# Self-attention with a fused 1x1 convolution: chunk 7's keys, chunk 6's and 7's scores and the turns of the maxima in another order

## The chip, the cores and the metric

One core of one Trainium2 chip runs the whole kernel. The metric is the device time of one execution in microseconds (us). TensorE does the matrix products into PSUM, VectorE (DVE) and ScalarE (ACT) copy, subtract and exponentiate, GpSimd (POOL) subtracts maxima, SyncE (SP) issues the transfers.

## What is computed

The input is four images of 256 channels and 64 x 64 = 4096 positions. The reference, cut to what matters:

```
xf = x.reshape(b, c, n)                     # 4, 256, 4096
q, k = Wq xf + bq, Wk xf + bk               # 32 channels each
v = Wv xf + bv                              # 256 channels
att = softmax(q^T k / sqrt(32), axis=-1)    # 4096 x 4096 per image
out = gamma * (v att^T)
result = Wf concat([out, x]) + bf           # 256 channels
```

All in float32. The kernel folds the first half of Wf and gamma into Wv, so that attention gives its part of the result at once, and computes the second half of Wf on x (the "convolution") while it reads x.

## The kernel before, in words

**Numbers in two parts.** Each float32 operand of a product is split into a high part, which a copy to a reduced format (fp32r) gives, and a low part, the rest, which DVE subtracts. A product is then three: high by high, high by low and low by high (`product3`). For keys and queries the parts are stacked on partitions, so that one product of 96 rows does all three.

**Two stages for each image.** `images` loops over the four images: projection of image 0, then a loop of three rounds (attention of image b, projection of image b + 1), then the attention of the last image. So the attention of image 0 follows the entry into the loop, those of images 1 and 2 follow the jump back to its head, that of image 3 follows the exit.

*Projection* goes over 8 chunks of 512 positions. A chunk has, on TensorE: the projection to keys and queries (6 products of 512 columns into `ps_p[:, 0]`), the four value tiles (each 6 products of 256 columns; tiles 0 and 1 into one bank of `ps_o`, tiles 2 and 3 into the other), two convolutions (6 products of 512 columns each), and one or two sets of "early scores". The other engines follow: ACT copies the high part of the next chunk's x (`split_x`), of keys and queries (`kq_hi`), of values (`values_out`), and stores the convolutions (`conv_out`); DVE makes the low parts (`split_x`, `kq_lo`, `values_lo`). `hi` and `lo` have two places, by chunk parity.

*Early scores.* A set of scores is four products of 256 columns (512 keys against a block of 256 queries), in two halves of two products. Each half takes one of three PSUM banks of `ps_s`. ACT copies it to `raw` (`keep_scores`), and then DVE folds it into a running maximum (`fold_scores`). On TensorE half h of `scores` waits until `max_done` has counted h - 2 folds, that is for the fold of half h - 3 (halves are numbered from 0), whose bank it takes; so three halves are under way at most. The sets are numbered in the order in which they are made (`MADE`): the set of chunk 6 has number 10 (halves 20 and 21), that of chunk 7 number 11 (halves 22 and 23).

*The maxima.* When all sets of block 0 are folded, `reduce_top` joins two running maxima to `top_j`; TensorE turns it into columns (`turn_top`, two transposes into `ps_t`); DVE reduces them to `top_col` (`reduce_turned`); TensorE turns and spreads that over all partitions (`spread_top`, two transposes); ACT copies it to `top_m` (`keep_top`); DVE subtracts it from the first slot of `raw` (`subtract_first`), and ACT makes the first exponential of it (`exponential_hi`), with which the attention begins. POOL subtracts it from the other slots.

*Attention* goes over 16 blocks of 256 queries, 8 steps each: per step 24 products of values with exponentials and 4 products of scores for 12 steps ahead.

**Order.** There is no planner. Each engine works through its own instructions in the order in which the code writes them, and semaphores, counted up by each piece, hold it: `k_out` and `q_out` tell that the low (and so both) parts of a chunk's keys and queries are there and that `ps_p[:, 0]` is free, `x_split` that a chunk's x is split, `v_free` that a bank of `ps_o` is free, `conv_ready` that a convolution is complete. The last convolution of chunk 7 goes into a bank of `ps_s`.

SP's queue: in chunk c it loads chunk c + 2 after the split of chunk c + 1 is done, then stores the two convolutions of chunk c.

Of the kernel before, what the change touches and what calls it, by code (L numbers as in the profile page):

```python
# [14 lines left out]
def attention_conv(nc, x, wkqT, wv, wf1T, wf2T, vectors, out):  # L15
# [4 lines left out]
    CHUNKS = N // W  # L20
    JT = N // P
    JC = W // P
# [30 lines left out]
    with ExitStack() as ctx:  # L53
# [163 lines left out]
        def _(pe):  # L217
# [70 lines left out]
            def project(b, c, first):  # L288
                C = snap(pe, b * CHUNKS + c)
                start = first and c == 0  # L290
                finishing = not first and c == 0
                last_chunk = c == CHUNKS - 1

                def project_kq(c, C):
                    pe.wait_ge(x_split, C + 1)
                    product3(ps_p[:, 0], lambda k: wkq_hi[:, k], lambda k: wkq_lo[:, k],
                             lambda k: x_hi(c)[:, k, :], lambda k: x_lo(c)[:, k, :]).then_inc(kq_ready, 1)

                def convolve(dst, ot, halfway=None):
                    product3(dst, lambda k: wf2_hi[:, k, ot * P:(ot + 1) * P],  # L300
                             lambda k: wf2_lo[:, k, ot * P:(ot + 1) * P],
                             lambda k: x_hi(c)[:, k, :], lambda k: x_lo(c)[:, k, :], halfway).then_inc(conv_ready, 1)

                def project_values(j):
                    if j % 2 == 0:
                        pe.wait_ge(v_free, C * 2 + (j // 2 + 1))
                    last = product3(ps_o[:, j // 2, (j % 2) * C_IN:(j % 2 + 1) * C_IN],
                                    lambda k: x_hi(c)[:, k, j * P:(j + 1) * P], lambda k: x_lo(c)[:, k, j * P:(j + 1) * P],
                                    lambda k: wvf_hi[:, k], lambda k: wvf_lo[:, k])
                    if j % 2:  # L310
                        last.then_inc(v_ready, 1)

                def early_scores(q):
                    scores(b * HALVES, MADE[q], 2 * MADE[q] % BANKS, q % QUADS, q // QUADS)

                if last_chunk:
                    pe.wait_ge(k_out, C + 1)
                    early_scores(c)
                    for j in range(JC):
                        project_values(j)  # L320
                    turn_top(b * BLOCKS, None)
                    pe.wait_ge(q_out, C + 1)
                    convolve(ps_p[:, 0], 0, lambda: spread_top(b * BLOCKS))
                    convolve(ps_s[:, LAST_CONV].rearrange("p j i -> p (j i)"), 1)
                    return
                if start:
                    warm_up()
                    pe.wait_ge(wkq_split, 1)
                elif finishing:
                    pe.wait_ge(lo_done, b * STEPS)  # L330
                else:
                    pe.wait_ge(k_out, C)
                project_kq(c, C)
                if start:
                    fold_weights()
                    pe.wait_ge(wf2_split, 1)
                    convolve(ps_t[:], 0)
                    pe.wait_ge(wvf_split, 1)
                    pe.wait_ge(ones_done, 1)
                if finishing:  # L340
                    turn_out(b * BLOCKS)
                project_values(0)
                project_values(1)
                if not start:
                    if finishing:
                        pe.wait_ge(finished, b * BLOCKS)
                    else:
                        pe.wait_ge(conv_done, C * 2)
                    convolve(ps_t[:], 0)
                project_values(2)  # L350
                project_values(3)
                pe.wait_ge(k_out, C + 1)
                pe.wait_ge(q_out, C + 1)
                if c in BETWEEN:
                    early_scores(BETWEEN[c])
                if c == CHUNKS - 2:
                    early_scores(c)
                    project_kq(c + 1, C + 1)
                    convolve(ps_p[:, 1], 1)
                else:  # L360
                    convolve(ps_p[:, 1], 1)
                    early_scores(c)

            def attend(b, n, r, last_image):
                B = snap(pe, b * BLOCKS + n)
# [78 lines left out]
        def _(act):  # L444
# [21 lines left out]
            def project(b, c, first):  # L466
# [26 lines left out]
                def early_scores(q):  # L493
                    keep_scores(b * HALVES, MADE[q], 2 * MADE[q] % BANKS, q)

                if last_chunk:
                    early_scores(c)
                    conv_out(ps_p[:, 1], 1, C - 1)
                    values_out(0)
                    values_out(1)  # L500
                    keep_top(b * BLOCKS, 0)
                    conv_out(ps_p[:, 0], 0)
                    act.wait_ge(sub0_done, b + 1)
                    exponential_hi(0, 0)
                    act.wait_ge(conv_done, C * 2 + 1)
                    exponential(b * STEPS, 0, 0)
                    conv_out(ps_s[:, LAST_CONV].rearrange("p j i -> p (j i)"), 1)
                    return
                if start:
                    split_x(0, 0)  # L510
                    act.wait_ge(wf2_loaded, 16)
                    nc.scalar.activation(wf2_hi[:], wf2_raw, ACT.Copy).then_inc(wf2_hi_done, 1)
                    act.wait_ge(vec_loaded, 16)
                    act.wait_ge(bkq_spread, 1)
                kq_hi(c, C)
                if start:
                    act.wait_ge(wvf_ready, 1)
# [3 lines left out]
                    act.wait_ge(pv_done, b * STEPS)  # L521
                elif not start:
                    act.wait_ge(conv_ready, C * 2)
                split_x(b, c + 1)
                values_out(0)
                conv_out(ps_t[:], 0)
                values_out(1)
                if c in BETWEEN:
                    early_scores(BETWEEN[c])
                if c == CHUNKS - 2:  # L530
                    early_scores(c)
                    kq_hi(c + 1, C + 1)
                else:
                    conv_out(ps_p[:, 1], 1)
                    early_scores(c)

            def exponential_hi(t, slot):
                nc.scalar.activation(hi[:, t % 2], raw[:, slot].rearrange("p j i -> p (j i)"), ACT.Exp,  # L538
# [34 lines left out]
        def _(dve):  # L573
# [83 lines left out]
            def project(b, c, first):  # L657
# [22 lines left out]
                    fold_scores(b * HALVES, MADE[q], 2 * MADE[q] % BANKS, None if q % QUADS == 0 else q // QUADS, q // QUADS)  # L680

                if last_chunk:
                    early_scores(c)
                    reduce_top(b * HALVES + 2 * MADE[c] + 2)
                    values_lo(0)
                    reduce_turned(b * BLOCKS)
# [8 lines left out]
                if finishing:  # L695
                    normalise(b * BLOCKS - 1, 1)
                    add_conv(b * BLOCKS - 1, 0, b * (16 * USES[0]))
                kq_lo(c, C)
                if start:
                    setup_values()  # L700
                split_x(C + 1, c + 1)
                values_lo(0)
                values_lo(1)
                if c in BETWEEN:
                    early_scores(BETWEEN[c])
                early_scores(c)
                if c == CHUNKS - 2:
                    kq_lo(c + 1, C + 1)

            def attend(b, n, r, last_image):  # L710
                B = snap(dve, b * BLOCKS + n)
# [98 lines left out]
```

## Time and profile before

| | us |
|---|---|
| median of 3 runs (2033.78 to 2034.09) | 2033.83 |
| the profiled execution, its own time | 2033.3 |
| its span, first to last instruction | 2031.4 |
| TensorE products busy | 2015.3 (99%) |
| TensorE weight loads busy | 1980.4 (97%) |
| ScalarE busy | 1748.9 (86%) |
| VectorE busy | 1584.9 (78%) |
| GpSimd busy | 1206.1 (59%) |

The 16 transfer engines move 34 GB/s on average. Two thirds of the chain of work that ended last are products of values in the attention. The projections of the four images lie at about 3 to 75, 514 to 579, 1018 to 1084 and 1523 to 1588 us. Products are pipelined, and their recorded durations overlap, so the distance between two starts is what one costs in a dense stretch.

### The profile page before, as it was taken

How to read it: one execution, taken by the hardware profiler on the slowest of the kernel's cores; microseconds unless marked ns; L12 is line 12 of the kernel's file. 1: busy time of each engine (PE TensorE's matmuls, PEld its weight loads, DVE VectorE, ACT ScalarE, POOL GpSimd, SP SyncE). 2: the span in 40 equal slices, each digit the busy share in tenths (PEclk: the TensorE clock that was granted, in tenths of full speed). 3: DMA queues.
4: the chain of work that ended last, by engine and by line, in shares of the span. 5: the costliest groups of instructions: out<-in, count | busy, mean ns of one | idle time of the engine just before them, and what ended most of it. 6: DMA issues, size and time to landing. Idle time of an engine off the chain costs nothing.

```text
span 2031.4 us, 45017 instructions
## 1 busy us (share of the span) xinstructions
PE 2015.3 (99%) x16232; PEld 1980.4 (97%) x16232; DVE 1584.9 (78%) x2157; ACT 1748.9 (86%) x2373; POOL 1206.1 (59%) x514
## 2 busy tenths in 40 slices
PE   9999999999999999999999999999999999999999
PEld 8999999999899999999989999999998999999999
DVE  6788888886778888888677888888867788888885
ACT  7888888887888888888788888888878888888886
POOL 0467766667056677666605666766660666677665
PEclk9999999999999999999999999999999999999999
DMA  4200000000310000000031000000003100000000
GB/s 136 84 22 22 15 15 21 21 21 12 120 70 22 22 21 15 16 21 21 11 125 65 22 21 21 21 10 21 21 11 130 38 22 21 21 21 18 13 21 17
DMA packets 54081, 69.46 MB, mean 34 GB/s; under 512 B 4048, under 2 KB 37584, under 8 KB 53968
## 3 DMA queue, kind: packets, MB, share of 16 engines
q1 hardware_dynamic: 53696, 67.91, 10.0%
q8 instruction: 68, 1.11, 0.2%
q14 instruction: 45, 0.37, 0.1%
q10 hardware_dynamic: 272, 0.07, 0.0%
HBM read 34.41 MB, written 33.55 MB: 33 GB/s over the span
## 4 chain that ended last, share of the span: by engine, by line
PE 92%; DVE 3%; ACT 3%; issue 2%; DMA 0%; DVEq 0%; ACTq 0%; SPq 0%
PE ps_o L388 72%; PE ps_s L380 11%; PE ps_p L242 3%; PE ps_o L242 2%; PE ps_t L284 1%; ACT queries L478 1%; ACT hi L453 1%; DVE val_lo L676 1%; PE ps_s L259 1%; PE ps_t L276 1%; PE ps_t L269 1%; DVE top L612 1%; DVE lo L599 1%; PE ps_t L242 0%; DVE raw L626 0%
## 5 line engine op out<-in xcount | busy, mean ns | idle before, releaser
L755 POOL TENSOR_TENSOR raw<-raw,top_m 128x1024 f32<-128x1024 f32 x508 | 1205.4, 2413 | 809.1 <-ACT top_m L464 809.1
L631 DVE TENSOR_TENSOR lo<-ps_p,hi 128x1024 fp32r<-128x1024 f32 x512 | 626.9, 1224 | 311.4 <-ACT ps_p L545 311.1
L612 DVE TENSOR_TENSOR top<-ps_s,top 128x512 f32<-128x512 f32 x960 | 660.0, 687 | 55.6 <-ACT raw L459 7.4
L538 ACT ACTIVATE hi<-raw 128x1024 fp32r<-128x1024 f32 x512 | 543.9, 1062 | 145.9 <-PE ps_o L388 141.4
L388 PE MATMUL ps_o<-val_hi,hi 128*128 128x258 f32 x4096 | 664.5, 284 | 4.1 <-ACT hi L538 4.1
L388 PE MATMUL ps_o<-val_lo,hi 128*128 128x256 f32 x4096 | 652.4, 281 | 0.0
L459 ACT ACTIVATE raw<-ps_s 128x512 f32<-128x512 f32 x1024 | 554.1, 595 | 54.7 <-PE ps_s L380 32.0
L388 PE MATMUL ps_o<-val_hi,lo 128*128 128x258 f32 x4096 | 599.3, 284 | 0.0
L388 PEld LDWEIGHTS ps_o<-val_hi,hi 128*128 128x128 f32 x4096 | 562.4, 189 | 5.8 <-issue 4.6
L388 PEld LDWEIGHTS ps_o<-val_lo,hi 128*128 128x128 f32 x4096 | 560.4, 189 | 0.0
L388 PEld LDWEIGHTS ps_o<-val_hi,lo 128*128 128x128 f32 x4096 | 538.7, 190 | 0.0
L545 ACT ACTIVATE ps_p<-raw 128x1024 f32<-128x1024 f32 x512 | 516.7, 1009 | 0.0
L380 PE MATMUL ps_s<-queries,keys 96*128 (+1 forms) x1856 | 306.7, 287 | 0.0
L380 PEld LDWEIGHTS ps_s<-queries,keys 96*128 96x128 f32 x1856 | 253.9, 190 | 0.1
L242 PE MATMUL ps_o<-wvf_hi,hi 128*128 128x256 f32 x256 | 72.0, 281 | 0.2 <-DVE bias L593 0.2
L242 PE MATMUL ps_o<-wvf_hi,lo 128*128 128x256 f32 x256 | 71.6, 280 | 0.0
L242 PE MATMUL ps_o<-wvf_lo,hi 128*128 128x256 f32 x256 | 71.5, 279 | 0.0
L643 DVE TENSOR_SCALAR o_norm<-ps_o,inv 128x256 f32<-128x256 f32 x128 | 61.9, 484 | 6.3 <-DVE inv L639 1.1
L242 PEld LDWEIGHTS ps_o<-wvf_hi,hi 128*128 128x128 f32 x256 | 48.0, 188 | 3.0 <-DVE bias L593 0.6
L242 PEld LDWEIGHTS ps_o<-wvf_lo,hi 128*128 128x128 f32 x256 | 48.1, 188 | 2.3
L649 DVE TENSOR_TENSOR result<-ps_t,result 128x512 f32<-128x512 f32 x64 | 43.6, 681 | 5.8 <-PE ps_t L284 5.8
L242 PEld LDWEIGHTS ps_o<-wvf_hi,lo 128*128 128x128 f32 x256 | 48.0, 188 | 0.0
(72 smaller groups left out, 1028.3 us busy)
## 6 DMA issues: line engine op xcount, KB each, us to landing
xf<-x SPq DMA_DIRECT2D x32, 512.0 KB, 3.7
conv_d<-conv_st SPq DMA_DIRECT2D x64, 256.0 KB, 2.0
result<-conv_d SPq DMA_DIRECT2D x64, 256.0 KB, 2.6
out<-result SPq DMA_DIRECT2D x64, 256.0 KB, 2.2
raw<-wf2T SPq DMA_DIRECT2D x1, 256.0 KB, 3.9
raw<-wv SPq DMA_DIRECT2D x1, 256.0 KB, 4.3
raw<-wf1T SPq DMA_DIRECT2D x1, 256.0 KB, 4.7
raw<-wkqT ACTq DMA_DIRECT2D x1, 64.0 KB, 2.0
```

What stands on the lines that cost most here:

```text
L242: last = nc.tensor.matmul(dst, a(k), b(k), start=(i == 0), stop=(i == len(terms) - 1))
L259: last = nc.tensor.matmul(ps_s[:, (bank + half) % BANKS, jl], keys[:, j * P:(j + 1) * P], queries[:, bass.ds(n * I, I)], start=True, stop= ...
L380: last = nc.tensor.matmul(ps_s[:, (2 * (QUADS * r + a) + half) % BANKS, jl], keys[:, j * P:(j + 1) * P], queries[:, bass.ds((n + a // QUAD ...
L388: last = nc.tensor.matmul(ps_o[:, i, 0:width], p[:, t % 2, jl * I + i * P:jl * I + (i + 1) * P], v[:, j, 0:width], start=opens and jl == 0 ...
L459: nc.scalar.activation(raw[:, slot, 2 * half:2 * half + 2], ps_s[:, (bank + half) % BANKS], ACT.Copy).then_inc(raw_done, 1)
L538: nc.scalar.activation(hi[:, t % 2], raw[:, slot].rearrange("p j i -> p (j i)"), ACT.Exp, scale=SCALE).then_inc(hi_done, 1)
L545: nc.scalar.activation(ps_p[:].rearrange("p h n -> p (h n)"), raw[:, slot].rearrange("p j i -> p (j i)"), ACT.Exp, scale=SCALE).then_inc(p ...
L612: nc.vector.tensor_tensor(top[:, new], scores, top[:, new if half else old], ALU.max).then_inc(max_done, 1)
L631: nc.vector.tensor_tensor(lo[:, t % 2], ps_p[:].rearrange("p h n -> p (h n)"), hi[:, t % 2].bitcast(F32), ALU.subtract).then_inc(lo_done, 1)
L643: nc.vector.tensor_scalar(o_norm[:, i], ps_o[:, i, 0:C_IN], inv[:, i:i + 1], None, ALU.mult).then_inc(o_scaled, 1)
L649: nc.vector.tensor_tensor(result[:, r], ps_t[:].rearrange("p (k n) -> p k n", k=KT), result[:, r], ALU.add).then_inc(finished, 1)
L755: nc.gpsimd.tensor_tensor(raw[:, slot], raw[:, slot], top_m[:, r].unsqueeze(1).broadcast_to((P, JQ, I)), ALU.subtract).then_inc(sub_done, 1)
```

## The change

All of it is in `project`, that is in the stage of projection, on TensorE, ACT and DVE. The counts and shapes of all operations stay.

In chunk 6, on TensorE: after the first convolution it waits for both parts of chunk 6's keys and queries, then comes chunk 7's projection, chunk 6's scores, value tiles 2 and 3, chunk 7's scores, and the second convolution. Before, value tiles 2 and 3 came right after the first convolution, then chunk 6's scores, chunk 7's projection and the second convolution; chunk 7's scores opened chunk 7.

In chunk 7, on TensorE: the turn of `top_j` stands between value tiles 1 and 2, the spreading of `top_col` behind tile 3, and both convolutions follow. Before, the turn stood behind tile 3 and the spreading half-way through the first convolution.

ACT and DVE take chunk 7's split in front of chunk 6's keys and queries, chunk 7's keys and queries in front of chunk 6's scores, and chunk 6's second pair of value tiles between the two sets of scores.

```
@@ TensorE, chunk 7
-                    pe.wait_ge(k_out, C + 1)
-                    early_scores(c)
-                    for j in range(JC):
-                        project_values(j)
+                    project_values(0)
+                    project_values(1)
                     turn_top(b * BLOCKS, None)
+                    project_values(2)
+                    project_values(3)
+                    spread_top(b * BLOCKS)
                     pe.wait_ge(q_out, C + 1)
-                    convolve(ps_p[:, 0], 0, lambda: spread_top(b * BLOCKS))
+                    convolve(ps_p[:, 0], 0)
                     convolve(ps_s[:, LAST_CONV].rearrange("p j i -> p (j i)"), 1)
@@ TensorE, the other chunks, behind the first convolution
+                if c == CHUNKS - 2:
+
+                    pe.wait_ge(k_out, C + 1)
+                    pe.wait_ge(q_out, C + 1)
+                    project_kq(c + 1, C + 1)
+                    early_scores(c)
+                    project_values(2)
+                    project_values(3)
+                    pe.wait_ge(k_out, C + 2)
+                    early_scores(c + 1)
+                    convolve(ps_p[:, 1], 1)
+                    return
                 project_values(2)
                 project_values(3)
                 pe.wait_ge(k_out, C + 1)
                 pe.wait_ge(q_out, C + 1)
                 if c in BETWEEN:
                     early_scores(BETWEEN[c])
-                if c == CHUNKS - 2:
-                    early_scores(c)
-                    project_kq(c + 1, C + 1)
-                    convolve(ps_p[:, 1], 1)
-                else:
-                    convolve(ps_p[:, 1], 1)
-                    early_scores(c)
+                convolve(ps_p[:, 1], 1)
+                early_scores(c)
@@ ACT
                 if last_chunk:
-                    early_scores(c)
                     conv_out(ps_p[:, 1], 1, C - 1)
...
+                if c == CHUNKS - 2:
+                    act.wait_ge(conv_ready, C * 2)
+                    split_x(b, c + 1)
                 kq_hi(c, C)
...
-                split_x(b, c + 1)
+                if c < CHUNKS - 2:
+                    split_x(b, c + 1)
                 values_out(0)
                 conv_out(ps_t[:], 0)
+                if c == CHUNKS - 2:
+                    kq_hi(c + 1, C + 1)
+                    early_scores(c)
+                    values_out(1)
+                    early_scores(c + 1)
+                    return
                 values_out(1)
                 if c in BETWEEN:
                     early_scores(BETWEEN[c])
-                if c == CHUNKS - 2:
-                    early_scores(c)
-                    kq_hi(c + 1, C + 1)
-                else:
-                    conv_out(ps_p[:, 1], 1)
-                    early_scores(c)
+                conv_out(ps_p[:, 1], 1)
+                early_scores(c)
@@ DVE
                 if last_chunk:
-                    early_scores(c)
                     reduce_top(b * HALVES + 2 * MADE[c] + 2)
...
+                if c == CHUNKS - 2:
+                    split_x(C + 1, c + 1)
                 kq_lo(c, C)
                 if start:
                     setup_values()
-                split_x(C + 1, c + 1)
+                if c < CHUNKS - 2:
+                    split_x(C + 1, c + 1)
                 values_lo(0)
+                if c == CHUNKS - 2:
+                    kq_lo(c + 1, C + 1)
+                    early_scores(c)
+                    values_lo(1)
+                    early_scores(c + 1)
+                    return
                 values_lo(1)
                 if c in BETWEEN:
                     early_scores(BETWEEN[c])
                 early_scores(c)
-                if c == CHUNKS - 2:
-                    kq_lo(c + 1, C + 1)
```

## Rows read from the trace of the kernel before

**Rows 1.** The page: busy time and share; the span in 40 slices, in tenths

```profile
PE 2015.3 (99%) x16232; PEld 1980.4 (97%) x16232; DVE 1584.9 (78%) x2157; ACT 1748.9 (86%) x2373; POOL 1206.1 (59%) x514
...
PE   9999999999999999999999999999999999999999
...
PEclk9999999999999999999999999999999999999999
```

**Rows 2.** Timeline, TensorE, image 0: start, us, engine, line, operation [idle before]

```profile
58.70 0.39 PE L242 MATMUL ps_p<-hi,wkq_hi 128*128 128x512 f32 x1
...
62.91 0.28 PE L242 MATMUL ps_o<-wvf_hi,hi 128*128 128x256 f32 x1
...
64.80 0.47 PE L242 MATMUL ps_p<-hi,wkq_hi 128*128 128x512 f32 x1
...
68.26 0.73 PE L259 MATMUL ps_s<-queries,keys 96*128 96x256 f32 x4 [0.43 <-DVE keys L665]
...
71.66 0.38 PE L269 MATMUL ps_t<-ident,top_j 128*128 128x128 f32 x2
...
72.57 0.42 PE L276 MATMUL ps_t<-ident,top_col 128*128 128x128 f32 x2
...
73.53 0.39 PE L242 MATMUL ps_s<-hi,wf_hi 128*128 128x512 f32 x1
...
75.89 0.76 PE L388 MATMUL ps_o<-val_hi,hi 128*128 128x258 f32 x4 [0.80 <-ACT hi L538]
```

**Rows 3.** The same timeline, ACT

```profile
58.63 1.08 ACT L459 ACTIVATE raw<-ps_s 128x512 f32<-128x512 f32 x2
60.29 0.68 ACT L475 ACTIVATE keys<-ps_p,bkkqq 64x512 fp32r<-64x512 f32 x1 [0.58 <-PE ps_p L242]
61.00 1.37 ACT L478 ACTIVATE queries<-ps_p,bkkqq 32x512 fp32r<-32x512 f32 x2
...
64.55 0.60 ACT L490 ACTIVATE val_hi<-ps_o 128x512 fp32r<-128x512 f32 x1
65.02 1.10 ACT L459 ACTIVATE raw<-ps_s 128x512 f32<-128x512 f32 x2
...
73.03 0.38 ACT L464 ACTIVATE top_m<-ps_t 128x256 f32<-128x256 f32 x1 [0.57 <-PE ps_t L276]
...
74.70 1.06 ACT L538 ACTIVATE hi<-raw 128x1024 fp32r<-128x1024 f32 x1 [0.28 <-DVE raw L626]
```

**Rows 4.** The same timeline, DVE

```profile
62.41 0.75 DVE L669 SCALAR_TENSOR_TENSOR queries<-ps_p,bkkqq,queries 32x512 fp32r<-32x512 f32 x1 [0.66 <-ACT queries L478]
...
64.74 1.29 DVE L676 TENSOR_TENSOR val_lo<-ps_o,val_hi 128x512 fp32r<-128x512 f32 x2
65.95 1.48 DVE L612 TENSOR_TENSOR top<-ps_s,top 128x512 f32<-128x512 f32 x2
...
70.95 0.42 DVE L617 TENSOR_TENSOR top_j<-top 128x256 f32<-128x256 f32 x1
...
72.08 0.42 DVE L621 TENSOR_REDUCE top_col<-ps_t 128x2 f32<-128x256 f32 x1
...
73.44 1.22 DVE L626 TENSOR_TENSOR raw<-raw,ps_t 128x1024 f32<-128x1024 f32 x1 [0.26 <-ACT top_m L464]
```

**Rows 5.** Load of chunk 7 of image 0: SP's timeline; issues with us to landing

```profile
50.80 0.43 SPq L160 DMA_DIRECT2D xf<-x  x1
...
xf<-x SPq DMA_DIRECT2D x1, 512.0 KB, 4.6
```

**Rows 6.** Timeline, TensorE's weight loads, the second half of chunk 5's scores

```profile
58.36 0.30 PEld L259 LDWEIGHTS ps_s<-queries,keys 96*128 96x128 f32 x2 [0.32 <-DVE top L612]
```

**Rows 7.** Timeline of image 1, TensorE and ACT, where its attention begins

```profile
578.77 0.40 PE L242 MATMUL ps_s<-hi,wf_lo 128*128 128x512 f32 x1
...
580.41 0.76 PE L388 MATMUL ps_o<-val_hi,hi 128*128 128x258 f32 x4 [1.24 <-ACT hi L538]
...
578.76 1.06 ACT L538 ACTIVATE hi<-raw 128x1024 fp32r<-128x1024 f32 x1 [0.20 <-DVE raw L626]
```

## The prediction

> **What bounds the kernel now.** The page first: TensorE is busy 99% of the span [rows 1]. I therefore ask of every edit one thing: at what time does TensorE begin the attention of the image, its long dense part? Work that is moved costs nothing and gives nothing unless that time moves. The change leaves the count and the shapes of all instructions as they are; only orders change, in chunks 6 and 7 of each of the four images.
>
> Next the timeline of the first image from chunk 6 on, one engine at a time [rows 2 to 4]. "A pair of value tiles" below is 12 products of 256 columns, "a convolution" and "the projection" are 6 products of 512 columns each. TensorE starts chunk 6's projection at 58.70 and the attention at 75.89, 17.19 us. The pieces: from 58.70 to 62.91 a projection, a pair and a convolution (4.21), from there to 64.80 a pair and the four score products (1.89; I take 1.41 and 0.48), so projection and convolution are 1.40 each. The whole of the two chunks is two projections, four convolutions, four pairs, two sets of scores and the two turns (0.14 and 0.18, my reading of what follows the rows at 71.66 and 72.57): 8.4 + 5.6 + 1.0 + 0.3 = 15.3 us. So 1.9 us are pauses, and they are: chunk 7's scores, which could have begun at 64.80 + 0.07 + 2 x 1.40 = 67.67 and begin at 68.26 when DVE has made the low part of the keys (0.6); the attention, which could have begun at 73.53 + 1.40 = 74.93 and begins at 75.89 when ACT has the first exponential (1.0); the rest is small seams. That, less than 2 us in an image, is all that this change can win.
>
> **The change part by part, first image.** Prices: raw copies of two score halves 1.10, the first of them done 0.60 after it starts and the second starting 0.50 after it; queries 1.37, keys 0.68, hi copy 1.06 (by the exponential, which has its shape), value copy 0.60 with the next start after 0.47 [rows 3]; on DVE queries 0.75 (the keys' low part has the same shape), two folds 1.48, so 0.69 for the first, two value subtractions 1.29 (0.65 each), top_j 0.42, column maxima 0.42, the 128x1024 subtraction 1.22 [rows 4]. Handing over from one engine to the next is some 0.05; a product's result is there 0.16 after the place at which the next could start (0.39 of the last minus its 0.23).
>
> *The split of chunk 7, moved ahead of chunk 6's keys.* ACT ends chunk 5's raw copies at 59.71 [rows 3], so the hi copy runs 59.7 to 60.8, keys to 61.5, queries 61.5 to 62.9. The convolution of chunk 5 that it waits for is long over by then, and the chunk's load was issued at 50.80 and such a load landed in 4.6 [rows 5], so nothing is added. DVE's 1.22 for the split lie beside ACT's keys and queries; its low part of the queries follows the copies, 62.9 to 63.7. In front of these copies everything is 0.5 later than before (the queries' copies began at 61.00).
>
> *Chunk 7's projection, moved ahead of the value tiles 2 and 3.* It overwrites the same PSUM bank, so it waits for that low part of the queries: ready at 62.91, it starts at 63.7. **Pause of 0.8 us**, new: before, 1.41 of value tiles and 0.48 of scores covered it. TensorE then runs projection and scores of chunk 6 to 65.6 and the pair to 67.0.
>
> *Chunk 7's scores in front of the second convolution.* Three PSUM banks hold scores, and the code lets a half start once the half three before it is folded and its bank so free (the max_done wait in scores). The halves of chunk 7 are numbers 22 and 23; 23 wants the fold of number 20, the first half of chunk 6. Follow that one: the projection is complete at 65.3; ACT now does chunk 7's keys (65.3 to 66.0) and queries (to 67.4) *before* it copies chunk 6's scores, so raw 20 is there at 68.0; DVE is in the low part of the queries until 68.15 and folds 20 until 68.9. TensorE has the keys in time (66.8), does half 22 from 67.0 to 67.2, and stands before half 23 until 68.95. **Pause of 1.7 us**, new. Convolution and value tiles are queued behind it, in order, and the score copy of 23, hence the maxima, too. That such a wait really holds TensorE is in the trace: chunk 5's second half stood 0.32 for exactly this releaser, the fold of the half three before [rows 6].
>
> *What is no longer between the turns.* From 68.95: half of the scores, the convolution and the first pair, to 72.0. DVE: fold 21 to 69.7, value tile to 70.3, folds 22 and 23 to 71.8, top_j to 72.2; the first turn starts at 72.3 (**pause 0.3**). Tiles 2 and 3 end at 73.8. Column maxima: ACT copies the first pair at 72.2 to 72.8, DVE subtracts it until 73.5, then reduces until 73.9; the second turn at 73.9 to 74.1 (**pause 0.1**). Two convolutions end at 74.1 + 2.81 = 77.0 with a seam.
>
> *The first exponential.* Before, second turn to top_m took 0.46, top_m to DVE's subtraction 0.41, that 1.22, and the exponential 1.06 with the hand-overs: 72.57 to 75.89, 3.3 in all [rows 2 to 4]. Now ACT and DVE have the second pair of value tiles in between (ACT until 74.5, DVE until 75.3; before, the low values were done before top_m). So top_m at 74.5 to 74.9, subtraction 75.3 to 76.5, exponential 76.6 to 77.6, attention at **77.7** instead of 75.89: **+1.8 us**. The change takes away the 0.6 at the keys and 0.2 of the 1.0 before the attention, and puts in 0.8, 1.7, 0.3 and 0.1: by pauses +2.1, less some seams; the two ways agree within 0.3, and I take 1.8 as it follows the last wait.
>
> *The other images.* Image 3 looks like image 0. Images 1 and 2 begin with the jump back to the head of the loop over images: in image 1 the exponential is done at 579.82, the last product starts at 578.77, and attention starts only at 580.41, 1.64 after that product starts, 1.41 after its place in the queue is free [rows 7]. There the start follows the end of the second convolution, 77.0 against 74.93, plus the same 1.41: **+2.0 us**. The exponential (77.6 on the clock of image 0, against 78.4) stays hidden. [...]
>
> Nothing is given back later. TensorE is dense after 75.89, and the exponentials of the next steps stand in the same distance to the start as before. Stores of the convolutions are issued up to 2 us later, and their results are wanted tens of us on.
>
> **Sum**: 2 x 1.8 + 2 x 2.0 = 7.6 us. Profiled execution 2033.3 to 2040.9; the median of the runs is 0.5 above it, so 2033.83 + 7.6 = **2041.4 us**, +0.37%.
>
> **The rivals.**
> Forecast, as worked out, chance 0.86. Its own range: hand-overs and overlapping tails (0.1 here and there over some ten steps) make 0.3 to 0.5 in an image, so 2039.5 to 2043.5.
> (a) *Only one pause counts*, 0.06. If ACT, which gets its conditions early, had the raw copy of half 20 a microsecond sooner than I schedule, the 1.7 shrinks to 0.7 and each image loses about 0.8 to 1.0: 2033.83 + 3.6 = 2037.4, at the edge of "same". For it: tails overlap on ACT (raw half starts 0.5 after the other). Against: keys and queries on ACT are 2.05 in one row after the other, with no overlap.
> (b) *The other sign*, 0.04: the fold of half 20 comes before TensorE asks. It decides whether that fold ends before 67.2, 1.7 earlier than I find, and then TensorE would have no hole at the keys and the turns hidden under convolutions. The gain is what pauses there are: 0.6 + 1.0 in images 0 and 3, and 0.6 in 1 and 2 where the jump remains, 4.4 together: 2029.4. What speaks against it is the order on ACT, raw copies behind keys and queries, and that fold and projection wait for nothing that could be early.
> (c) *It is absorbed*, 0.02: later starts are caught up in attention, 2034. TensorE is at 9 tenths in all slices [rows 1], there is nothing to catch up with.
> (d) *The clock*, 0.02. [...]
>
> **The numbers.** A measurement of this kernel can tell about 0.2% (4.1 us) from no change. Slower by more: forecast, (d) and a little of (a), 0.88. Within it: most of (a), (c), 0.08. Faster: (b), 0.04. Range, 8 in 10: below down to (a)'s 2037.5, above by the upper end of the step errors plus half a microsecond an image for seams I can't see, 2044.
>
> **What would show it.** In the profile after: a wait of TensorE of some 0.7 to 0.8 before a product into ps_p, released by DVE's low part of the queries; a wait of ps_s for DVE top near 1.7 in each image, the largest new one; the wait for DVE keys gone; top_col and top_j with waits of 0.1 to 0.3; the attention of image 0 at 77.7. I am wrong if the wait for the fold is under 1 us, if the attention starts before 76.5, or if waits of the same size turn up within the attention.

## The result, and the profile after

| | before | after |
|---|---|---|
| median of the runs, us | 2033.95 | 2042.12 |
| lowest to highest | 2033.78 to 2034.09 | 2042.01 to 2042.24 |
| span of the profiled execution | 2031.4 | 2040.1 |

The changed kernel is slower, by 8.2 us: ratio 1.004, 95% interval 1.0027 to 1.0053. The forecast was 2041.4 with a range of 2037.5 to 2044.0, so the sign and the size were right. By the spans of the two profiled executions the difference is 8.7, as the one of before (2033.3 us) is 0.65 below the median of its kernel.

The timeline of the changed kernel in image 0, TensorE; it answers to [rows 2]. In this execution chunk 6 starts at 58.81 and not at 58.70, so everything is 0.1 later than in the one of before ahead of the change.

```profile
63.70 0.47 PE L242 MATMUL ps_p<-hi,wkq_hi 128*128 128x512 f32 x1 [0.51 <-issue]
...
67.07 0.40 PE L259 MATMUL ps_s<-queries,keys 96*128 96x256 f32 x2
69.02 0.51 PE L259 MATMUL ps_s<-queries,keys 96*128 96x256 f32 x2 [1.55 <-DVE top L625]
...
72.26 0.44 PE L269 MATMUL ps_t<-ident,top_j 128*128 128x128 f32 x2
...
74.08 0.43 PE L276 MATMUL ps_t<-ident,top_col 128*128 128x128 f32 x2
...
77.83 0.75 PE L396 MATMUL ps_o<-val_hi,hi 128*128 128x258 f32 x4 [0.51 <-ACT hi L551]
```

The lines show the two new holes. Chunk 7's projection could have started at 63.02, 0.23 behind the last product ahead of it, and starts at 63.70, when DVE has the low part of chunk 6's queries (62.85 + 0.75 below): a hole of 0.7. The second half of chunk 7's scores, number 23, starts at 69.02 and not 0.24 behind the first at 67.07: from 67.31 the engine stands for 1.7 us. The idle time in brackets is 1.55, as it counts from the recorded end of the last product, 67.47. The wait is put down to DVE's fold. The next fence has the same stretch on ACT and then on DVE, for [rows 3, 4].

```profile
66.09 1.37 ACT L486 ACTIVATE queries<-ps_p,bkkqq 32x512 fp32r<-32x512 f32 x2
67.48 1.08 ACT L467 ACTIVATE raw<-ps_s 128x512 f32<-128x512 f32 x2
...
74.64 0.38 ACT L472 ACTIVATE top_m<-ps_t 128x256 f32<-128x256 f32 x1
...
76.64 1.06 ACT L551 ACTIVATE hi<-raw 128x1024 fp32r<-128x1024 f32 x1
...
62.85 0.75 DVE L682 SCALAR_TENSOR_TENSOR queries<-ps_p,bkkqq,queries 32x512 fp32r<-32x512 f32 x1
...
68.27 1.49 DVE L625 TENSOR_TENSOR top<-ps_s,top 128x512 f32<-128x512 f32 x2
...
71.78 0.42 DVE L630 TENSOR_TENSOR top_j<-top 128x256 f32<-128x256 f32 x1
...
75.39 1.21 DVE L639 TENSOR_TENSOR raw<-raw,ps_t 128x1024 f32<-128x1024 f32 x1
```

ACT copies chunk 7's queries from 66.09 and starts the score copies only behind them, at 67.48, so the first is there at about 68.08. DVE makes the low part of the queries from 67.49 to 68.24 and folds from 68.27; the first fold ends at 68.96, 0.06 before half 23. The waits of the whole run, who waited for whom (total, times, longest):

```profile
PE ps_s L259 <- DVE top L625: 6.2, 4, 1.6
...
ACT hi L551 <- POOL raw L774: 2.8, 2, 1.5
```

The first is the new hole, once in each of the four images. The second was not forecast; it belongs to the attentions of images 1 and 2. Image 1 in the timeline of the changed kernel, TensorE and then ACT (for [rows 7]):

```profile
582.87 0.40 PE L242 MATMUL ps_s<-hi,wf_lo 128*128 128x512 f32 x1
583.95 0.74 PE L396 MATMUL ps_o<-val_hi,hi 128*128 128x258 f32 x4 [0.69 <-ACT hi L551]
...
587.78 0.75 PE L396 MATMUL ps_o<-val_hi,hi 128*128 128x258 f32 x4 [0.21 <-ACT hi L551]
...
590.55 0.51 PE L388 MATMUL ps_s<-queries,keys 96*128 96x256 f32 x2 [0.35 <-DVE top L625]
...
584.50 0.67 ACT L494 ACTIVATE conv_st<-ps_s,bias 128x512 f32<-128x512 f32 x1
586.66 1.06 ACT L551 ACTIVATE hi<-raw 128x1024 fp32r<-128x1024 f32 x1 [1.49 <-POOL raw L774]
```

and the kernel before at the same place, ACT, then TensorE:

```profile
580.67 0.67 ACT L486 ACTIVATE conv_st<-ps_s,bias 128x512 f32<-128x512 f32 x1
582.10 1.06 ACT L538 ACTIVATE hi<-raw 128x1024 fp32r<-128x1024 f32 x1 [0.75 <-issue]
...
583.88 0.65 PE L388 MATMUL ps_o<-val_hi,hi 128*128 128x258 f32 x4
```

The second exponential of the attention is the first instruction of ACT behind the jump to the head of the loop. Before, it started 1.43 after the convolution's copy and was done at 583.16, in time for TensorE's second step at 583.88. After, it starts 2.16 behind the copy, is done at 587.72, and TensorE's second step, 3.47 behind the first in the kernel before, comes 3.83 behind it. The scores of that step then wait 0.35 for a fold of DVE (590.55), and behind them the whole 1.0 is lost: the next products start at 590.89 and before at 586.33, 4.56 apart, where the attentions start 3.54 apart. That POOL is named is no proof: POOL's subtraction for this slot began at 581.16 and takes 2.4, so it was done three microseconds before.

**Where 8.7 us of span went**, from the start of an attention and the start of the next projection (75.89, 513.78, 580.41, 1018.34, 1085.03, 1523.10, 1589.22 before; 77.83, 515.71, 583.95, 1022.91, 1091.07, 1529.94, 1597.93 after). Projections until the attention starts: +1.94, +1.61, +1.47, +1.87. Attentions: 0.0, +1.03, +0.80, 0.0. Together 8.7.

### The profile page after: what moved, and what is told of

It reads as the page before. It is cut to its first block, busy times and chain, and to the rows that moved or that the text cites. A ratio compares the mean times of both kernels' runs of the same rounds, so it can differ in the third digit from the quotient of the medians.

```text
span 2040.1 us, 45018 instructions
## 1 busy us (share of the span) xinstructions
PE 2018.3 (99%) x16232; PEld 1981.4 (97%) x16232; DVE 1584.6 (78%) x2157; ACT 1748.6 (86%) x2373; POOL 1205.9 (59%) x514
## 3 DMA queue, kind: packets, MB, share of 16 engines
q8 instruction: 68, 1.11, 0.2%
## 4 chain that ended last, share of the span: by engine, by line
PE 92%; ACT 3%; DVE 3%; issue 2%; DMA 0%; ACTq 0%; DVEq 0%; SPq 0%
PE ps_o L396 72%; PE ps_s L388 11%; PE ps_p L242 3%; PE ps_o L242 2%; PE ps_t L284 1%; ACT queries L486 1%; ACT hi L461 1%; PE ps_t L242 1%; PE ps_t L269 1%; DVE lo L612 1%; PE ps_s L259 1%; PE ps_t L276 1%; DVE val_lo L689 1%; DVE top L625 0%; DMA xf<-x 0%
## 5 line engine op out<-in xcount | busy, mean ns | idle before, releaser
L242 PE MATMUL ps_o<-wvf_hi,hi 128*128 128x256 f32 x256 | 72.3, 282 | 0.2 <-DVE bias L606 0.2
L689 DVE TENSOR_TENSOR val_lo<-ps_o,val_hi 128x512 fp32r<-128x512 f32 x64 | 42.3, 688 | 8.3 <-ACT val_hi L498 6.9
```

What stands on the lines that cost most here:

```text
L242: last = nc.tensor.matmul(dst, a(k), b(k), start=(i == 0), stop=(i == len(terms) - 1))
L689: nc.vector.tensor_tensor(val_lo[:, j2, :], ps_o[:, h].rearrange("p (j c) -> p j c", j=2), val_hi[:, j2, 0:C_IN].bitcast(F32), ALU.subtrac ...
```

## The experiments

The kernel before ran on the same chips, with medians of 2033.88 to 2034.02. The names are those of the first kernel's stages; "the changed kernel" is the one of the diff.

**1. Chunk 7's scores behind the second convolution.** Does TensorE's hole of 1.7 us cost 1.7 us?

```
                     pe.wait_ge(k_out, C + 2)      # moved, with early_scores(c + 1),
+                    convolve(ps_p[:, 1], 1)       # behind the convolution
                     early_scores(c + 1)
```

> The changed kernel, with chunk 7's scores behind chunk 6's second convolution on TensorE. Theory 1 (the chain through the queues of ACT and DVE sets the start of the attention, and TensorE's long pause only shows it): half 23 starts at about 69.0 as before this edit, because the fold of half 20 is no earlier; the pause of 1.7 shrinks to 0.3, but an equal one of about 1.6 appears before the turn of top_j, and the attention of image 0 starts at 77.5 to 77.8; total 2041 to 2042. Theory 2 (TensorE's pause is the loss): 1.4 us come back in each image, total about 2036.5.

Measured: 2041.76 us (ratio to before 1.0037, 1.0024 to 1.0051). The hole did shrink, and came back in front of the turn, where TensorE now waits for top_j:

```profile
72.32 0.44 PE L269 MATMUL ps_t<-ident,top_j 128*128 128x128 f32 x2 [1.38 <-DVE top_j L630]
```

The attention of image 0 starts at 77.89. Removing the longest wait of TensorE brought 0.4 us in all, hardly more than the scatter of the runs (2041.55 to 2042.20 here, 2042.01 to 2042.24 for the changed kernel). By the traces images 0 and 3 gain nothing (from projection to attention 77.89 and 68.01, where the changed kernel has 77.83 and 67.99); what there is lies in images 1 and 2, behind the jump. What sets the end is the chain over ACT's and DVE's queues; the hole only shows where TensorE meets it.

**2. Chunk 7's queries last on ACT and DVE.** The same chain, cut at its cause. `kq_hi` and `kq_lo` are divided into keys and queries:

```
@@ ACT, chunk 6
-                    kq_hi(c + 1, C + 1)
+                    k_hi(c + 1, C + 1)
                     early_scores(c)
                     values_out(1)
                     early_scores(c + 1)
+                    q_hi(c + 1, C + 1)
@@ DVE: k_lo in chunk 6; in chunk 7
                     reduce_top(b * HALVES + 2 * MADE[c] + 2)
+                    q_lo(c, C)
```

> The changed kernel, with chunk 7's queries taken on ACT behind both sets of scores and on DVE behind top_j; TensorE's order as it is. Theory 1 (the fold of half 20 is late because its raw copy is queued behind the 1.4 us of query copies): half 20 is folded at 67.5 instead of 69.0, the pause before half 23 is 0.3, top_j at 70.8, the attention of image 0 at about 76.3 (77.83 in the changed kernel, 75.89 before); total about 2036. Rival (the fold waits for something else, the projection or DVE's own queue): the pause stays over 1 us and the total at 2041 or more.

Measured: 2036.50 us (1.0011, 1.0002 to 1.0020): 5.6 of the 8.2 us come back. TensorE, then DVE, image 0:

```profile
67.70 0.50 PE L259 MATMUL ps_s<-queries,keys 96*128 96x256 f32 x2
70.95 0.44 PE L269 MATMUL ps_t<-ident,top_j 128*128 128x128 f32 x2
...
76.53 0.74 PE L396 MATMUL ps_o<-val_hi,hi 128*128 128x258 f32 x4 [0.50 <-ACT hi L554]
...
66.95 1.49 DVE L628 TENSOR_TENSOR top<-ps_s,top 128x512 f32<-128x512 f32 x2
```

The fold starts at 66.95 instead of 68.27, half 23 at 67.70 instead of 69.02, both 1.32 earlier, and the attention 1.30 earlier. One delay runs through the chain undiminished. The edit moved two things at once, ACT's copies of the queries (1.37) and DVE's low part of them (0.75); what each of them costs alone was not measured. In the changed kernel DVE's part ended last (68.24, the raw copy at 68.08), but it had waited for ACT's copies to end.

**3 and 4. The loop over images written out**, in the changed kernel and in the one before. No engine jumps between a projection and an attention:

```
-            with eng.Fori(0, IMAGES - 1) as b:
+            for b in range(IMAGES - 1):
```

> The changed kernel with the loop over images written out, so that no engine jumps back between the projection and the attention of images 1 and 2. Theory 1 (the jump delays TensorE's start and ACT's second exponential of the attention): images 1 and 2 behave as image 0; the losses within the attention (1.0 and 0.8 us found between its start and the next projection) go, and 0.25 at each start; total about 2040. Rival (these losses come from the later start itself, as from the transfers that now meet): they stay, total 2042.

> The kernel before with the loop over images written out. Theory 1: the attentions of images 1 and 2 start when the exponential is there, 0.5 to 0.6 earlier each: total about 2032.8. Rival (longer code costs reads of instructions elsewhere, or the 1.4 us were no jump): 2034 or more.

Measured: 2038.92 us for the changed kernel (1.0022, 1.0013 to 1.0031) and 2031.59 for the one before (0.9987, 0.9978 to 0.9996), 1 us better than expected in both. The attentions of images 1 and 2, from their start to the next projection, take 437.96 and 437.97 in the changed kernel written out, where they took 438.96 and 438.87; the one before takes 437.94 in both. ACT, image 1 of the changed kernel written out:

```profile
584.23 0.67 ACT L494 ACTIVATE conv_st<-ps_s,bias 128x512 f32<-128x512 f32 x1
584.80 1.05 ACT L551 ACTIVATE hi<-raw 128x1024 fp32r<-128x1024 f32 x1
```

The second exponential starts 0.57 behind the copy, where it was 2.16 with the loop. So the time lost within the attention belonged to the jump. The attention of image 0 speaks for the jump itself and not for anything else in the loop's code: it is that same code, entered without a jump, and takes 437.8 to 437.9 in every kernel with the loop. Without jumps the change costs 7.3 us instead of 8.2, and it costs nearly the same in each image: the attention starts 1.86, 1.78, 1.77 and 1.77 later, counted from the projection. That is the 1.8 which the prediction had for image 0.

**5. Value tiles 2 and 3 back in front of chunk 7's projection.** The other hole, in front of that projection:

```
                 if c == CHUNKS - 2:
+                    project_values(2)
+                    project_values(3)
                     pe.wait_ge(k_out, C + 1)
                     pe.wait_ge(q_out, C + 1)
                     project_kq(c + 1, C + 1)
                     early_scores(c)
-                    project_values(2)
-                    project_values(3)
```

> The changed kernel with value tiles 2 and 3 of chunk 6 back in front of chunk 7's projection on TensorE, so that they cover the wait for the low part of the queries. Theory 1 (the chain from chunk 7's projection over ACT's and DVE's queues to the first exponential sets the start): the pause of 0.5 to 0.8 before that projection goes, but the projection starts at 64.3 instead of 63.7, and everything behind it is 0.6 later, the attention of image 0 at 78.4; total about 2044.5. Theory 2 (each pause of TensorE is a loss of its own): 0.7 us come back in each image, total about 2039.

Measured: 2049.99 us (1.0080, 1.0066 to 1.0094). The sign is that of theory 1, the size is of neither. TensorE, image 0, and the windows of that stretch (busy time and count of each engine, granted clock, share and rate of transfers):

```profile
67.72 0.50 PE L259 MATMUL ps_s<-queries,keys 96*128 96x256 f32 x2 [1.07 <-DVE keys L677]
69.84 0.79 PE L259 MATMUL ps_s<-queries,keys 96*128 96x256 f32 x2 [1.62 <-DVE top L624]
70.43 0.63 PE L242 MATMUL ps_p<-hi,wf_hi 128*128 128x512 f32 x1
70.86 0.63 PE L242 MATMUL ps_p<-lo,wf_hi 128*128 128x512 f32 x1
...
75.55 0.50 PE L269 MATMUL ps_t<-ident,top_j 128*128 128x128 f32 x2
```

```profile
64.00:70.00 6.00, 3.31 (x20) 2.62 (x18) 2.76 (x5) 3.97 (x8) 0.00 (x0) 0.91 0.12 44
70.00:76.00 6.00, 6.00 (x23) 5.42 (x24) 2.89 (x5) 1.87 (x4) 0.00 (x0) 0.52 0.12 44
```

The chain is late by a little more than the 0.6 expected: half 23 starts at 69.84, 0.8 behind the changed kernel. But the products behind it start 0.43 apart instead of 0.233. The granted clock of this stretch is 0.52, where it is 1.00 over 58 to 64 and over 76 to 82 us. The wider distance lasts until about 75.6, and the convolution and two value tiles between 70.43 and 75.55 took 5.1 us instead of 2.8. Ahead of that it had stood 1.07 and 1.62, with two products in between. Images 2 and 3 have such a stretch too, of some 3 us (0.57 and 0.72 in windows of 4 and 6 us). Image 1 has not, though its two waits are the same (1.14 and 1.55; 1.15 and 1.55 in image 2, 1.14 and 1.55 in image 3). In image 1 it is 68.95 from the start of the projection to that of the attention, 0.7 more than the 68.24 of the changed kernel: 4 x 0.7 on 2042 is 2045, near what theory 1 expected. Images 0, 2 and 3 are later by another 2.6, 1.7 and 1.1 in the same stage, and these 5.4 us go with the lower clock.

**6. The turns alone, on the kernel before.**

```
-                    for j in range(JC):
-                        project_values(j)
+                    project_values(0)
+                    project_values(1)
                     turn_top(b * BLOCKS, None)
+                    project_values(2)
+                    project_values(3)
+                    spread_top(b * BLOCKS)
                     pe.wait_ge(q_out, C + 1)
-                    convolve(ps_p[:, 0], 0, lambda: spread_top(b * BLOCKS))
+                    convolve(ps_p[:, 0], 0)
```

> The kernel before with this part of the change alone: the turn of top_j between value tiles 1 and 2, the spreading behind tile 3. From the rows of before: top_j is ready at 71.4 and TensorE at 70.2, a pause of 1.2; spreading at 73.0 (72.57 before), then ACT and DVE have the second pair of value tiles in front of top_m and of the subtraction, attention of image 0 at about 76.8, +0.9; in images 1 and 2, where the jump hides half of it, +0.45. Total 2034 + 2.7 = about 2036.7. Rival (the turns cost nothing where they are put, as the waits that they meet are short): 2034.

Measured: 2038.46 us (1.0023, 1.0014 to 1.0032), 4.5 more than before, where 2.7 was expected. TensorE waits 1.02 for top_j, the spreading comes at 73.22, and the attention of image 0 starts at 77.10, 1.2 later than before. It was expected to cost 0.9 in two images and 0.45 in two. By the traces it costs 1.2, 1.5, 1.3 and 1.1: in images 1 and 2 only 0.6 of it shows at the start of the attention, and another 0.9 and 0.7 are lost behind the jump, where nothing was expected.

**7. The spreading back into the convolution, in the changed kernel.**

```
-                    spread_top(b * BLOCKS)
                     pe.wait_ge(q_out, C + 1)
-                    convolve(ps_p[:, 0], 0)
+                    convolve(ps_p[:, 0], 0, lambda: spread_top(b * BLOCKS))
```

> The changed kernel with the spreading of the maxima back half-way in the first convolution of chunk 7, at about 74.5 instead of 74.08 in image 0. For the jump: if TensorE's start behind it counts from the last wait that TensorE passes (3.8 us after the spreading in both kernels), the attention of image 1 starts 0.5 later than in the changed kernel, at 584.4; if it counts from the end of the last convolution, it starts at 583.9 as there. The first exponential waits for DVE's second value tile in any case, so image 0 stays within 0.1 of 77.83. Total 2042 to 2042.5.

Measured: 2041.85 us (1.0039, 1.0024 to 1.0055). The attention of image 1 starts at 584.06, with the spreading at 580.77, so 3.3 behind it and not 3.8: the start does not count from the last wait. (Image 0, expected within 0.1 of 77.83, starts at 78.00.) But nor does it keep a fixed distance to the last product, which is 1.64 and 1.70 before and 1.08 and 1.00 after.

**8. An order made by the chain, loop written out.** Taken from kernel 2 of this list (that of experiment 2), with the following on TensorE, and the other queues as the expectation says:

```
@@ chunk 6
                     project_values(2)
                     project_values(3)
                     pe.wait_ge(k_out, C + 1)
                     pe.wait_ge(q_out, C + 1)
                     project_kq(c + 1, C + 1)
                     early_scores(c)
                     convolve(ps_p[:, 1], 1)
                     pe.wait_ge(k_out, C + 2)
                     early_scores(c + 1)
@@ chunk 7
                     project_values(3)
                     turn_top(b * BLOCKS, None)
                     spread_top(b * BLOCKS)
```

> An order made by the chain: loop over images written out; on TensorE value tiles 2 and 3 of chunk 6, chunk 7's projection, chunk 6's scores, the second convolution as cover for chunk 7's keys, chunk 7's scores, its four value tiles, both turns, both convolutions; ACT and DVE take chunk 7's queries behind both sets of scores, DVE the column maxima before the value tiles and the first subtraction before the last. Theory 1: no pause at the keys, 0.3 before half 23, top_j at 70.8 instead of 71.4 and the attention of image 0 at 75.4 (75.89 before, 75.80 with the loop written out); total about 2030. Rival (the chain has another step that I don't see, and nothing comes of it): 2031.6 as the written-out loop alone, or more.

Measured: 2031.57 us (0.9988, 0.9979 to 0.9997), the same as the kernel before with the loop written out. The maxima came earlier, and another instruction took the gain. Its ACT, image 0:

```profile
72.81 0.39 ACT L471 ACTIVATE top_m<-ps_t 128x256 f32<-128x256 f32 x1 [0.32 <-PE ps_t L276]
74.22 0.69 ACT L494 ACTIVATE conv_st<-ps_p,bias 128x512 f32<-128x512 f32 x1 [1.02 <-PE ps_p L242]
74.80 1.05 ACT L553 ACTIVATE hi<-raw 128x1024 fp32r<-128x1024 f32 x1
```

DVE's subtraction is done at 74.45, and the exponential could start at 74.5, but ACT had begun the copy of the convolution, which this order made late enough to be in the way. The attention starts at 75.90, where 75.4 was expected and the kernel before written out has 75.80; this copy cost 0.3 of the 0.5 that are missing. It was not tried to turn these two round: the low part of the same exponential would wait for that copy.

**9. The rest of the change alone.** The changed kernel with both turns where they were.

```
-                    turn_top(b * BLOCKS, None)
                     project_values(2)
                     project_values(3)
-                    spread_top(b * BLOCKS)
+                    turn_top(b * BLOCKS, None)
                     pe.wait_ge(q_out, C + 1)
-                    convolve(ps_p[:, 0], 0)
+                    convolve(ps_p[:, 0], 0, lambda: spread_top(b * BLOCKS))
```

> The changed kernel with the turns of the maxima where they were before (behind tile 3, and half-way in the first convolution): the rest of the change alone. From the rows of the changed kernel: half 23 still starts at 69.0, the value tiles end at 73.6, turn at 73.6, top_col at 74.5, spreading at 74.6, top_m to 75.4, subtraction and exponential after it, attention of image 0 at 77.9 to 78.0. The turns alone cost 4.5 us in all. If the parts add up, the rest alone costs the other 3.7: total about 2037.7. If each part fills the other's wait (both chains end in the same first exponential), it costs as much as the whole: about 2042.

Measured: 2041.13 us (1.0039, 1.0025 to 1.0053), 7.2 over the kernel before. The attention of image 0 starts at 77.70. Turns 4.5, rest 7.2, both 8.2: the two delays lie beside each other, they don't add. Images 1 and 2 are worth a look here. Their attentions start 2.0 and 1.9 later than before, counted from the projection, 1.79 and 1.67 behind the start of the last product, and take 437.93 and 438.03: nothing is lost within them. So with the turns in their old places the kernel does what the prediction said of the jump. In all seven kernels here with the loop and the turn of top_j between value tiles 1 and 2, these attentions take 438.3 to 439.0. Why the place of the turn should matter to what comes behind the jump is not shown.

**10. Queries last, and value tiles back.** Kernel 2 with the edit of kernel 5.

> Chunk 7's queries last on ACT and DVE, as in the run that brought the most back, and value tiles 2 and 3 of chunk 6 back in front of chunk 7's projection, as in the run in which TensorE's clock fell. The chain: projection at 64.4, keys' low part at 67.5, fold of half 20 at 68.2, half 23 at 68.3 (67.70 without the tiles moved back), turn 71.6, attention of image 0 at 77.1; pauses of 1.2 and 0.5 us instead of 1.1 and 1.6. If the clock fell because of the long pauses close together, it stays at 1.00 here and the total is about 2038.7; if the place of the value tiles itself brings it down, the clock falls here too and the total is 2045 or more.

Measured: 2040.42 us (1.0034, 1.0022 to 1.0046), with runs from 2038.48 to 2041.70, wider than any other kernel's here. The profiled run is the 2038.48 one: half 23 at 68.18, turn at 71.43, attention at 77.01, 0.1 to 0.2 ahead of the expected times, and the granted clock is 1.00 over 60 to 80 us. So in this execution, with waits of 1.07 and 0.22, the clock held, and the time is the 2038.7 expected for that case. The other five are 1.3 to 3.2 us longer, and the two longest (2041.48 and 2041.70) have a mean clock of 0.998 against 0.999. That would fit a clock that falls in one or two images, but no trace shows it; the median lies between the two expectations and decides for neither.

**11. The turns alone, loop written out.**

> The turns alone, with the loop over images written out. If the 0.9 us which the attentions of images 1 and 2 lose behind a later start come from the jump, they go, and the cost of the turns is 1.2 us in each image and nothing else: 2031.6 (the kernel before written out) + 4.8 = 2036.4. If they come from something that the late turns disturb, about 2038.

Measured: 2036.10 us (1.0011, 1.0002 to 1.0020), 4.5 over the kernel before written out. The attentions take 437.96 and 437.96 again, and start 1.2, 1.1, 1.1 and 1.1 later than there with what went before taken off.

## Why the prediction was right

*The hole before chunk 7's projection, 0.8.* Right in place and cause: the projection starts at 63.70, forecast 63.7. As 0.1 was there before, the hole is 0.7.

*The hole before half 23, 1.7, by the fold of half 20.* Right in place, cause and size: 69.02, forecast 68.95. The cause (raw copies queued behind the query copies) is shown by experiment 2, which took the queries out of both queues and moved the fold and half 23 and the attention by the same 1.3.

*Turns and first exponential.* Turn 72.26 (72.3), spreading 74.08 (73.9), exponential 76.64 (76.6), attention 77.83 (77.7), of which 0.1 was there before the change. The two small waits ahead of the turns were 0.1 each, where 0.3 and 0.1 were forecast. That image 0 costs 1.8 was no luck: with the loop written out all four images cost 1.8 to 1.9 (experiments 3 and 4). The two ways of adding up, by waits and by the last wait, were put side by side in the prediction, as they agreed within 0.3, and it took the second. Experiments 1 and 5 say that they are not equals: a wait of TensorE that is taken away comes back in front of the next thing that the chain delivers (1), or delays the chain (5). Only the sum along the chain is a forecast.

*Images 1 and 2.* Here a step failed. The prediction took 1.41 us from the end of the last convolution to the attention as a constant, +2.0 at each start, and said that nothing would be lost within the attention. Measured were +1.6 and +1.5 at the starts, and 1.0 and 0.8 lost behind them, as ACT came back from the jump 2.2 and 2.0 after the copy instead of 1.4 and 1.6. Kernels 3 and 4 show that it is the jump, and kernel 9 that the constant holds as long as the turns are where they were. The prediction's own sign of being wrong, new waits within the attention, did turn up there: 1.5 and 1.3 on ACT, and 0.2 to 0.4 on TensorE. The term was 4.0 for both images and measured 4.9; that is most of the difference between 7.6 and 8.2 or 8.7 us. The range held it, with its half a microsecond an image for what could not be seen; the reason itself was not foreseen.

*The rivals.* That one hole alone counts, that the delay is absorbed, or that the kernel is faster: none happened. The clock did not fall in the changed kernel, whose single long wait is 1.55, with 1.00 in the windows of all four projections. In experiment 5 it did fall, to 0.52 over 70 to 76 us of image 0: 2.8 us of products took 5.1 there, and the attention started another 2.6 us later.

**Open.** What in the jump makes ACT late by 2.2 rather than 1.4, and what TensorE's start behind it counts from. Experiment 7 excluded both simple rules; experiment 9 ties it to the place of the turns, without a reason. Also what takes TensorE's clock down in three of four images of kernel 5 and not in the other, with the same two waits.

## What to carry to other kernels

Where the dense engine has pauses of 1 to 2 us in a hand-written order, find the chain of the other engines' queues that sets the next dense stretch, and add up along it. The longest wait of the dense engine is where it meets that chain; moving work into the wait brought 0.4 of 1.7 x 4 us, moving 1.4 us of ACT's copies and 0.75 of DVE's out of the chain, in each image, brought 5.6. If two long waits come close together (1.07 and 1.62 us in image 0 of kernel 5, with a granted clock of 0.52 behind them), look at the granted clock before explaining the time. A loop that runs three times and jumps at a place where engines wait for each other can be written out: that gave 2.4 us here, the only gain found over the kernel before.

## What the runs showed of the hardware that was not expected

TensorE's granted clock went from 1.00 to 0.50 in three images of kernel 5, after two waits with two products between them: from 69.84 to 75.60 us in image 0 (waits of 1.07 and 1.62), from 1086.26 to 1089.46 in image 2 (1.15 and 1.55) and from 1595.18 to 1598.15 in image 3 (1.14 and 1.55), that is for 5.8, 3.2 and 3.0 us from the start of half 23 on. Products of 512 columns were 0.43 apart in it, and 0.233 apart in image 0's next convolution. It did not always: image 1, with 1.14 and 1.55, kept 1.00. One wait of 1.54 or 1.55 alone (the changed kernel), or of 1.33 to 1.38 (experiment 1), left it at 1.00 in all images.

Behind the jump to the head of the loop, TensorE's first product came 1.6 and 1.7 us behind the start of its last one in the kernel before, 1.1 and 1.0 in the changed one; with the loop written out it was 1.11 in the kernel before and 0.83 in the changed one. ACT's second exponential came 1.4 and 1.6 us behind the start of its last copy before, 2.2 and 2.0 in the changed kernel, and 0.57 in both with the loop written out. So the delay on ACT went with the jump; what the engine does in that time no run shows.
